# When the last stage's expert weights are loaded: two in the last batch and six behind the last store, ahead of the rows

## The reference, cut to what matters

```python
x = x + tanh(g_xattn[0]) * L0_xattn(layernorm(x), ctx, mask)        # 16 heads of 16
x = x + tanh(g_ffn[0])   * L0_ffn(layernorm(x))                     # small experts, top 2 of 8
x = x + tanh(g_xattn[1]) * L1_xattn(ctx, layernorm(x), mask)        # 16 heads of 64, 487 keys
x = x + tanh(g_ffn[1])   * L1_ffn(layernorm(x))                     # large experts, top 2 of 8

def L1_ffn(xf):                                  # 1792 tokens of 256, H = 512
    logits = xf @ Wr + br
    val, idx = top_k(logits, 2); scores = softmax(val)
    h = einsum('nd,edh->enh', xf, W1) + b1       # a, g = two halves of h
    out_e = einsum('enh,ehd->end', silu(a) * g, W2) + b2
    return sum(out_e at idx, weighted by scores)
```

## Time and profile before

| | us |
|---|---|
| median of 3 runs | 1396.94 (1396.32 to 1399.18) |
| the profiled execution | 1397.87 |
| its span | 1396.1 |
| mean granted clock of TensorE | 0.944 of full speed |
| PE busy | 1224.2 (88% of the span) |
| DVE busy | 1080.9 (77%) |
| ACT busy | 996.9 (71%) |
| POOL busy | 813.6 (58%) |
| DMA queue q1 (SP) | 140.82 MB, 46.8% of 16 engines |
| DMA queue q0 (POOL) | 35.80 MB, 10.4% |

### The profile page before, as it was taken

How to read it: one execution, slowest core, us unless ns; L and a number is a source line. 1 busy time by engine, 2 the same in 40 slices (tenths; PEclk the granted TensorE clock), 3 DMA queues, 4 the chain that set the end, 5 groups by cost and what they waited for, 6 DMA issues and landing times. The chain is left out here.

```text
span 1396.1 us, 38073 instructions
## 1 busy us (share of the span) xinstructions
PE 1224.2 (88%) x13060; PEld 878.1 (63%) x13060; DVE 1080.9 (77%) x3112; ACT 996.9 (71%) x2552; POOL 813.6 (58%) x1204
## 2 busy tenths in 40 slices
PE   5899999999985599999999999999999974489994
PEld 3677777777763245666656666656666653388994
DVE  4899999999984268888888888888888882477772
ACT  4888888888873368888787888787888771256662
POOL 3545445455423445777777777777777674146564
PEclk8899999999997699999999999999999985699998
DMA  6546455344310149777688877888777693853323
GB/s 185 149 135 176 121 158 165 110 136 144 105 51 21 42 97 164 152 141 152 140 158 163 157 141 149 139 159 162 157 136 153 139 197 58 323 150 57 61 36 76
DMA packets 309406, 185.50 MB, mean 133 GB/s; under 512 B 257930, under 2 KB 295186, under 8 KB 306112
## 3 DMA queue, kind: packets, MB, share of 16 engines
q1 hardware_dynamic: 293024, 140.82, 46.8%
q0 software_dynamic: 13168, 35.80, 10.4%
q10 hardware_dynamic: 3024, 6.47, 1.6%
HBM read 76.19 MB, written 49.94 MB: 90 GB/s over the span
## 5 line engine op out<-in xcount | busy, mean ns | idle before, releaser
L1685 ACT ACTIVATE b_prob<-b_prob,b_top 112x487 f32<-112x487 f32 x256 | 178.8, 698 | 28.6 <-DVE b_top L1811 26.9
L1318 POOL TENSOR_TENSOR b_halves<-b_prob,b_halves 112x487 f16<-112x487 f32 x128 | 146.8, 1147 | 80.6 <-ACT b_halves L1710 79.2
L1496 PE MATMUL b_ps_p<-w_s,b_tok_s 128*128 128x512 f16 (+1 forms) x768 | 187.7, 381 | 4.0 <-DVE b_k_s L1798 3.2
L1496 PE MATMUL b_ps_p<-b_tok_s,w_s 128*128 128x487 f16 x768 | 183.1, 376 | 6.4 <-POOL b_tok_s L1312 3.7
L1811 DVE CUSTOM_DVE_ANT_0 b_prob<-b_ps_s,b_keep 112x487 f32<-112x487 f32 x256 | 167.4, 655 | 13.6 <-PE b_ps_s L1589 12.0
L721 ACT ACTIVATE a_prob<-a_prob,a_top 112x375 f32<-112x375 f32 x256 | 155.0, 606 | 5.4 <-DVE a_top L856 2.3
L1710 ACT ACTIVATE b_halves<-b_prob 112x487 f16<-112x487 f32 x256 | 155.9, 609 | 0.4
L856 DVE CUSTOM_DVE_ANT_0 a_prob<-a_ps_s,a_keep 112x375 f32<-112x375 f32 x256 | 138.2, 540 | 14.8 <-PE a_ps_s L614 14.6
L622 PE MATMUL a_ps_t<-a_const,a_prob 112*125 112x112 f32 x768 | 134.2, 284 | 12.7 <-ACT a_prob L721 10.4
L861 DVE TENSOR_TENSOR a_pT<-a_ps_t,a_pT 125x336 f16<-125x336 f32 x256 | 128.2, 501 | 20.5 <-ACT a_pT L728 19.5
L1604 PEld LDWEIGHTS b_ps_o<-b_v_s,b_pT 128*128 128x128 f16 (+1 forms) x3072 | 123.7, 99 | 31.9 <-DMA b_pT<-b_halves 12.0
(11 more groups left out here) (263 smaller groups left out, 3016.8 us busy)
## 6 DMA issues: line engine op xcount, KB each, us to landing
xs<-a_blank SPq DMA_DIRECT2D x14, 1032.0 KB, 4.2
c_w_pool<-w_split SPq DMA_DIRECT2D x8, 1600.0 KB, 10.1
b_wch_f<-in_w_experts POOLq DMA_DIRECT2D x32, 384.0 KB, 5.1
w_split<-b_wch_s POOLq DMA_DIRECT2D x32, 384.0 KB, 3.4
a_k_stack<-keys SPq DMA_DIRECT2D x96, 93.8 KB, 3.2
a_ctx_f<-in_ctxT SPq DMA_DIRECT2D x16, 375.0 KB, 3.9
keys<-a_k_s SPq DMA_DIRECT2D x16, 375.0 KB, 3.2
b_ctx_t<-in_ctx SPq DMA_DIRECT2D x16, 375.0 KB
```

The source lines that it names most:

```text
L1318: pool.tensor_tensor(halves[:, h % TURN, LO, 0:NK], prob[:, h % RING, 0:NK], halves[:, h % TURN, HI, 0:NK], ALU.subtract).then_inc(s_lo[1], 1)
L1496: last = pe.matmul(out, sta(a, k), mov(m, k), start=(k == 0 and n == 0), stop=(k == tiles - 1 and n == 2))
L1685: act.activation(prob[:, h % RING, 0:NK], prob[:, h % RING, 0:NK], ACT.Exp, bias=top[:, h % RING:h % RING + 1], scale=-1.0, accum_out=sums ...
```

## The change

The space of `w_pool` is reserved at the start of the program and is no longer an allocation of stage c. Stages a and b take a number of their own buffers out of it (`room`, `take`). In stage b these are, in this order, `k_s[0]`, `v_s[0]`, `k_s[1]`, `v_s[1]`, `halves`, `pT`, `tok_f`, `order` and `x2_n`. The buffers keep their sizes and types. Experts 0 and 1 take 12,800 two-byte elements of a partition, and `k_s[0]` with `v_s[0]` take 15,984, so these two experts lie on keys and values of the even batches alone.

SP then loads the experts in stage b. In the last batch it loads expert 0 in slot 7 and expert 1 in slot 9, each ahead of that slot's turn, once all values of batch 14 are computed. Experts 2 to 7 follow behind the last store, once all values of batch 15 are computed and the last weights are stored to `w_split`. Stage c loads no weights. There, SP announces expert i behind the rows of tile i, for the first eight tiles. The semaphores of the loads now belong to the whole program.

```diff
+            def load_expert(e):
+
+                need(sp, s_pv, H, B - 2 if e < 2 else B - 1, H)
+                if e >= 2:
+                    for j in range(2):
+                        sp.wait_ge(s_wchstore[j], 16 * B)
+                sp.dma_start(w_pool[:, e, :], w_dram[e]).then_inc(s_w[e], 16)
+
             def body(b, par):
                 for s in range(H):
+                    if not ahead(b, 1) and s in (7, 9):
+                        load_expert((s - 7) // 2)
...
             residual(B - 1)
             store(B - 1)
+            for e in range(2, E):
+                load_expert(e)
             sp.wait_ge(s_store, 16 * B)
...
-        w_pool = sb("w_pool", [128, E, SW], F16)
...
-            def load_expert(e):
-                sp.dma_start(w_pool[:, e, :], w_dram[e]).then_inc(s_w[e], 16)
-
-            load_expert(0)
             for i in range(TILES):
-                if i == 4:
-                    announce(0)
-                    load_expert(1)
-                elif i == 8:
-                    announce(1)
-                    load_expert(2)
-                    load_expert(3)
-                elif i == XT:
-                    for e in range(4, E):
-                        load_expert(e)
-                    announce(2)
-                if XT <= i < XT + E - AHEAD - 1:
-                    announce(i - XT + AHEAD + 1)
                 load(i)
+                if i < E:
+                    announce(i)
```

More of the change, by code:

```diff
@@ L12 @@
+import math
 from contextlib import ExitStack
@@ L63, with room, take @@
 BLANK = 128 * 8
+def room(tensor):
+    flat = tensor[:, :, :].rearrange("p e n -> p (e n)")
+    taken = [0]
+    def take(shape, dt):
+        n = math.prod(shape[1:]) * (2 if dt == F32 else 1)
+        part = flat[0:shape[0], taken[0]:taken[0] + n]
+        taken[0] += n
+        part = part.bitcast(F32) if dt == F32 else part
+        axes = "abcde"[:len(shape) - 1]
+        sizes = dict(zip(axes[1:], shape[2:]))
+        return part.rearrange("p (" + " ".join(axes) + ") -> p " + " ".join(axes), **sizes) if len(axes) > 1 else part
+    return take
 def need(eng, sem, per, batch, count, met=None):
@@ L103, in phase_attention_small_heads @@
 def phase_attention_small_heads(nc, x, ctxT, mask, g_xattn, g_ffn, wq, wk, wv, bq, bk, bv, wg, we, be, consts,
[L104 removed]
+                                x2_dram, next_w, next_w_dram, xs_dram, k_dram, q_dram, w_pool):
     with ExitStack() as ctx:
@@ L109, in phase_attention_small_heads @@
         sem = lambda name: ctx.enter_context(nc.semaphore("a_" + name))
+        take = room(w_pool)
         bank = lambda name: ctx.enter_context(nc.psum_tensor("a_" + name, [128, 512], F32))
@@ L114, in phase_attention_small_heads @@
         neg_half = sb("neg_half", [128, 1], F32)
-        wqkv_f = sb("wqkv_f", [128, KT, 3 * D + E], F32)
-        wqkv = sb("wqkv", [128, 2, KT, 3 * D + E], F16)
-        we_s = sb("we_s", [128, 2, KT, E * D], F16)
+        wqkv_f = take([128, KT, 3 * D + E], F32)
+        wqkv = take([128, 2, KT, 3 * D + E], F16)
+        we_s = take([128, 2, KT, E * D], F16)
         NEXT = next_w_dram.shape[1] // H
@@ L121, in phase_attention_small_heads @@
         WE = E * D // (H // 2)
-        next_f = sb("next_f", [128, next_w_dram.shape[1]], F32)
+        next_f = take([128, next_w_dram.shape[1]], F32)
         we_f = next_f[:, 0:KT * E * D].rearrange("p (k n) -> p k n", k=KT)
@@ L137, in phase_attention_small_heads @@
         tanhs = sb("tanhs", [128, 4], F32)
-        blank = sb("blank", [BLANK // 8, 8 * ROW], F32)
+        blank = take([BLANK // 8, 8 * ROW], F32)
         x_in = sb("x_in", [T, D], F32)
@@ L157, in phase_attention_small_heads @@
         Q_PARTS, K_PARTS = (HI, HI, LO), (HI, LO, HI)
-        q_stack = [sb(f"q_stack{i}", [2 * STACK, 2, H // 2, T], F16) for i in range(2)]
+        q_stack = [take([2 * STACK, 2, H // 2, T], F16) for i in range(2)]
         k_s = sb("k_s", [128, 2, 2, C], F16)
-        k_stack = [sb(f"k_stack{i}", [2 * STACK, H // 2, C], F16) for i in range(2)]
+        k_stack = [take([2 * STACK, H // 2, C], F16) for i in range(2)]
         v_s = [sb(f"v_s{i}", [128, NB0, H, 2, D0], F16) for i in range(2)]
         RING = 4
-        prob = sb("prob", [T, RING, C], F32)
+        prob = take([T, RING, C], F32)
         top = sb("top", [T, RING], F32)
         sums = [sb(f"sums{i}", [T, H], F32) for i in range(2)]
-        pT = sb("pT", [128, RING, 2, NB0, 128], F16)
+        pT = take([128, RING, 2, NB0, 128], F16)
         x_res = sb("x_res", [T, D], F32)
@@ L1013, in phase_attention_large_heads @@
                                 x2_dram, acc_dram, xs_dram, w_all, w_dram, b2_all, ones, cum, s_rows, head, s_head,
-                                ident_h, s_ident, b1_f):
+                                ident_h, s_ident, b1_f, w_pool, s_w):
     with ExitStack() as ctx:
@@ L1054, in phase_attention_large_heads @@
         q_s = [sb(f"q_s{i}", [128, 2, IT, T], F16) for i in range(2)]
-        k_s = [sb(f"k_s{i}", [128, 2, IT, NK], F16) for i in range(2)]
-        v_s = [sb(f"v_s{i}", [128, 2, NB1, INNER], F16) for i in range(2)]
+        k_s, v_s = zip(*((take([128, 2, IT, NK], F16), take([128, 2, NB1, INNER], F16)) for i in range(2)))
         RING = 4
@@ L1063, in phase_attention_large_heads @@
         TURN = 8
-        halves = sb("halves", [T, TURN, 2, NB1 * KB1], F16)
-        pT = sb("pT", [128, TURN, 2, NB1, 128], F16)
+        halves = take([T, TURN, 2, NB1 * KB1], F16)
+        pT = take([128, TURN, 2, NB1, 128], F16)
+        tok_f = take([128, KT, NK], F32)
+        order = take([T, T], F32)
+        x2_n = take([T, D], F32)
         x_res = sb("x_res", [T, D], F32)
@@ L1095, in phase_attention_large_heads @@
         both = sb("both", [T, E], F16)
-        order = sb("order", [T, T], F32)
         before = sb("before", [T, T], F16)
@@ L1936, with phase_experts @@
 TABLE_COUNT, TABLE_ROW = 4, 18
-def phase_experts(nc, w_dram, xs_dram, acc_dram, ones, cum, s_rows, head, s_head, ident, s_ident, b1_f, out):
+def phase_experts(nc, w_dram, xs_dram, acc_dram, ones, cum, s_rows, head, s_head, ident, s_ident, b1_f, w_pool, s_w, out):
     with ExitStack() as ctx:
@@ L1992, in phase_experts @@
         s_valid = sem("valid")
-        s_w = [sem(f"w{e}") for e in range(E)]
         s_x = [sem(f"x{i}") for i in range(XSEM)]
@@ L2297, in build_program @@
         s_rows = ctx.enter_context(nc.semaphore("rows"))
+        w_pool = ctx.enter_context(nc.sbuf_tensor("w_pool", [128, E, SW], F16))
+        s_w = [ctx.enter_context(nc.semaphore(f"w{e}")) for e in range(E)]
         with nc.sbuf_tensor("w1_s", [128, 2, WKV + WQ + WOUT], F16) as w1_s:
```

9 lines of the change are left out of this document (3 added, 6 removed).

## The result

The kernel before took 1396.94 us (median of five runs, 1396.03 to 1400.06), the changed one 1387.94 us (five runs, 1386.99 to 1390.67). The ratio is 0.9935 with a 95% interval from 0.9916 to 0.9954: faster by 0.65%, or 9.1 us. The prediction was 1386.5. The profiled execution took 1387.11 us, with a span of 1385.3 us, against 1397.87 and 1396.1 before.

A forecast was written before the change was run, and what follows sets the result against it. Taken as bound: stage c's serial chain of 35 scatters. Terms -7.5 (first scatter earlier), -7.2 (its landing) and +4.2 (last batch) give -10.5 from 1397.87, so 1387.4; less 0.9 for the median, 1386.5 us; range 1382 to 1391.

The forecast's parts named there:

- Rival C: Stage c: PE's tiles set the step for longer, so only the first scatter's gain counts; 1393.7 us, chance 0.07.
- Lent space: Buffers of stages a and b at other addresses, same shapes and instructions: cost 0.
- Six loads behind the last store: Experts 2 to 7 on SP's queue: first lands in 6.4 us, each further 4.1, expert 7 at 1199.8.
- Rows behind the loads: Start of stage c: tile 0's rows wait for all six loads, landing at 1200.7 against 1194.38, a 6.3 us loss.
- DVE's waits and ACT's silu: Stage c's start: waits of 8.81 and 5.22 us go, rows to product takes 4.0, first scatter 7.5 us earlier.
- The first scatter's landing: Stage c: with the DMA quiet, the second scatter follows after a plain step, 7.2 us gained.
- The barrier: Ahead of stage c: slowed scatters may hold it some 6 us more, hidden behind expert 7's load; price 0.
- rival B: End of stage b: SP's drain waits for its six loads, rows land 7.4 us later; 1393.9 us, chance 0.10.
- The last batch: End of stage b: loads of experts 0 and 1 delay turns on SP's queue; +4.2 us, range 1 to 8.
- Rival D: Last batch of stage b: turns never catch up, 5.3 us paid in four rounds, 21.2 us; 1403.5 us, chance 0.08.
- Rival A: Last batch of stage b: turns catch up in the eight-deep ring, 0 to 1 us later; 1382.8 us, chance 0.15.
- The sum: Whole kernel: -7.5 - 7.2 + 4.2 = -10.5 us against the profiled 1397.87, so 1387.4; by the median 1386.5.

The follow-up runs named there:

- the version with four loads at the tail: Changed kernel, but experts 0 to 3 load behind the last residual's load and ahead of the last store, 4 to 7 behind that store; 1383.2 us, ratio 0.9893.

## Why the prediction was right

**The bound** held: the scatters of stage c in series. Taking the sum out of them shortened the time by 0.76% of before. But the prediction read this bound from the last links of the chain of waits and from POOL's waits alone. Before, that chain runs through PE's tiles for most of stage c. The bound is a near tie, with PE's tiles 0.2 us a step behind. Rival C, that PE's tiles keep the scatters from starting earlier, is out, since the second scatter followed after 4.71 us and POOL then waited for landings.

**Lent space** at 0: shown by the kernel that has nothing else.

**Six loads behind the last store**: predicted 4.1 us each behind the first's 6.4. The first landed after 7.0 us and the further ones 3.9 us apart (longest landing 23.9 us). Two more moved the rows by 3.86 us each. The 423 GB/s of the earlier trace rows were the better basis than the nearest pair, and the windows after show 417 to 435. The Trainium skill, in DMA: Bandwidth & Descriptors, section Where 436 GB/s comes from, has about 358 GB/s for HBM to SBUF. By that figure a load would take 4.6 us, as an estimate; neither trace agrees.

**Rows behind the loads**: predicted at 1204.9, with the last batch's delay in it; they landed at 1204.57. The close hit is in part luck, as the stretch up to the last batch was 1.9 us shorter and the last batch 2.2 us dearer than foreseen; counted from the last store, 28.2 us were predicted and 27.6 measured. That the queue holds them, the kernel with eight loads ahead of them shows.

**DVE's waits and ACT's silu**: predicted 4.0 us from rows to product, measured 3.68. From product to first scatter 8.3 predicted, 9.38 measured. In the window of the product, 1205 to 1210, the clock was still granted at 0.50, after PE had stood nearly still from 1185 to 1205. I had taken 1.0 us off for a clock that rose only in the window after.

**The first scatter's landing**: predicted 7.2 us, measured 7.08. Its condition, a quiet DMA, was met in all kernels with all eight loads in stage b, whose next steps are 4.5 to 4.7 us. In the two that keep loads 4 to 7 behind the rows of tile 11, with lent space alone and with only 0 and 1 moved, it stayed at 12.2 and 11.8 us.

**The barrier**: POOL's drain grew by 4.0 us (up to 6 foreseen), SP's stayed at 13 ns with six loads under way. That refutes rival B. The delay was hidden behind expert 7, as predicted: the rows were issued at 1200.76, ahead of its landing at some 1204. The cover is thin. Of the 5.7 us by which the rows come later behind the store, a later issue accounts for 4.0 (23.8 us instead of 19.8), and only 1.7 are the queue's own. In the version with four loads at the tail the cover is gone, and the barrier sets the rows.

**The last batch** is the term that was mis-sized. The prediction had +4.2 us; these two profiles give +6.4, and the means of four loaded and five unloaded kernels give 54.8 - 49.1 = 5.7. The chain that I followed had PE standing 2 us for the turn behind expert 0 and then late by 4.2 us at the scores of heads 14 and 15. PE in fact stood 3.25 us behind the first load and 4.24 us behind the second, and it reached those scores 32.7 us into the batch instead of 25.5, so 7.2 us late. One load alone costs 1.7 us, and the second, issued before the first had landed, 4.0. Rival D, a delay paid again in every round, is out: 5.7 us lie under the 10.6 of both delays paid once, and far under 21.2. Rival A, that the ring swallows both loads, is refuted by the batch's marks and by what taking them out gained.

**The sum** by itself: -10.5 predicted, -10.8 in the profiled execution, -9.1 by the ratio. The near hit of the profiled execution is luck: it had 1.9 us in its favour up to the last batch, which isn't the change's, and that covers what the last batch cost above the forecast. Without it the profile gives -8.9, near the ratio. Of the 1.6 us between -10.5 and -8.9, the last batch has 1.5 to 2.2, by the means or by the two profiles.

## What to carry to other kernels

A hole in the DMA's timeline is worth filling up to the point where what is queued behind the fill is itself waited for; here six loads ahead of the rows cost 6 us and returned 20. Where a ring of small transfers is already waited for, a large one in the same stretch is paid by the ring and not by its bytes. Look for a stretch just behind it: here the same loads some 20 us later were free, and by the ratios this beat the change by some 4.7 us with two of them and 5.9 with four.

## What was not expected of the hardware

- Two loads of 1.6 MB on ACT's queue beside transposing transfers on SP's queue held the latter up so that PE stood for 17 us (the longest landed after 25.0 us, 3.2 being the median of the earlier trace rows). At the end of this time the DMA share was 1.3 to 1.8 with 75 to 148 GB/s moved. On SP's own queue, in order, the same two cost 6 us. One on ACT's queue cost 2.3.
- SP's drain took 13 ns with six of its transfers under way, while POOL's took 8.06 us, 4.0 more than before, when the DMA was full. So SP's drain doesn't cover its loads. That POOL's covers its scatters fits, as it took 8.1 to 9.1 us in all nine kernels with loads behind the store and 4.1 in the three without; but no view shows when those scatters landed.
- An accumulating scatter that took 11.0 us to land beside four loads takes 3.9 with the DMA quiet; without the accumulation the median is 2.4 instead of 3.8, and that takes only 0.2 us off the step, as PE's tiles come next.
